# Attention probabilities copied between strips of partitions: 32 rows of 4 KB against 32 rows of four 1 KB pieces

## The reference, cut to what matters

```
xn = layernorm(x)                                  # x: 8 x 1024 x 256, f32
q, k, v = split(einsum('bse,ehd->bshd', xn, w_qkv))  # 16 heads of 64
logits = einsum('bqhd,bkhd->bhqk', q, k) / 8, masked to k <= q
out = einsum('bhqk,bkhd->bqhd', softmax(logits), v)
result = x + einsum('bshd,hde->bse', out, w_out) + moe_ffn(xn)   # 8 experts, top 2
```

## Time and profile before

| | |
|---|---|
| median of 3 runs | 3329.88 us (3329.76 to 3335.65) |
| profiled execution, its own time | 3331.94 us |
| its span, first to last instruction | 3330.1 us |
| mean granted TensorE clock | 0.977 of full speed |
| TensorE busy | 3097.9 us (93%) |
| VectorE, ScalarE, GpSimd busy | 63%, 55%, 48% |
| attention stage | from about 945 us to the end |

### The profile page before, as it was taken

How to read it: one execution, slowest core, us unless ns; L and a number is a source line. 1 busy time by engine, 2 the same in 40 slices (tenths; PEclk the granted TensorE clock), 3 DMA queues, 4 the chain that set the end, 5 groups by cost and what they waited for, 6 DMA issues and landing times.

```text
span 3330.1 us, 62693 instructions
## 1 busy us (share of the span) xinstructions
PE 3097.9 (93%) x21140; PEld 2555.3 (77%) x21141; DVE 2094.2 (63%) x5279; ACT 1840.2 (55%) x4180; POOL 1605.0 (48%) x2256
## 2 busy tenths in 40 slices
PE   5489999999969999999999999999999999999997
PEld 3479998999957777777777777777777777777775
DVE  6844344444337677667766777777776776666665
ACT  3344444455426566656655666666665665556553
POOL 2132222122036565665556666666666655655553
PEclk9799999999979999999999999999999999999998
DMA  6122222112045656656565655656565565555553
GB/s 202 34 73 75 74 72 69 62 59 74 30 117 136 147 140 152 147 136 152 141 146 136 158 139 143 157 146 145 139 162 143 137 155 141 142 131 147 128 134 88
DMA packets 246206, 408.82 MB, mean 123 GB/s; under 512 B 69713, under 2 KB 170129, under 8 KB 245905
## 3 DMA queue, kind: packets, MB, share of 16 engines
q1 hardware_dynamic: 221328, 337.80, 40.4%
q0 software_dynamic: 24576, 67.14, 7.8%
HBM read 102.80 MB, written 33.55 MB: 41 GB/s over the span
## 4 chain that ended last, share of the span: by engine, by line
PE 29%; DVE 19%; SPq 14%; DMA 9%; issue 2%; POOL 0%; ACT 0%; DVEq 0%; POOLq 0%
SPq L1081 14%; PE O L1260 12%; PE S L1224 10%; DMA pT<-squares 8%; DVE squares L1385 8%; DVE S L1406 7%; PE T L1236 4%; DVE res L1372 2%; PE W L1181 2%; DVE negm L1406 1%; DVE ol L1390 1%; PE S L1148 1%; DMA ql<-kk 0%; DVE rinv L1351 0%; DMA kk<-qq 0%
## 5 line engine op out<-in xcount | busy, mean ns | idle before, releaser
L1485 POOL TENSOR_SCALAR pr<-pr,rinv 128x128 f32<-128x128 f32 (+7 forms) x1024 | 765.3, 748 | 868.6 <-DVE rinv L1351 861.9
L1304 ACT ACTIVATE pr<-S,negm 128x128 f32<-128x128 f32 (+7 forms) x1024 | 761.1, 743 | 716.9 <-DVE negm L1406 704.5
L1406 DVE CUSTOM_DVE_ANT_0 S<-S,late 128x128 f32<-128x128 f32 (+7 forms) x1024 | 777.3, 759 | 504.9 <-PE S L1224 504.8
L1260 PE MATMUL O<-pT,vv 128*64 128x256 f32 (+1 forms) x5120 | 587.6, 373 | 97.1 <-DMA pT<-squares 94.8
L1224 PE MATMUL S<-kk,qq 128*128 128x256 f32 (+2 forms) x1536 | 591.1, 385 | 13.7 <-DMA qq<-qq 8.7
L1260 PEld LDWEIGHTS O<-pT,vv 128*64 128x64 f32 x5120 | 348.3, 140 | 298.2 <-DMA pT<-squares 109.7
L1224 PE MATMUL S<-kk,ql 128*128 128x256 f32 (+2 forms) x1536 | 517.3, 344 | 0.0
L1236 PE MATMUL T<-ident,pr 128*128 128x128 f32 x2688 | 418.5, 272 | 0.3 <-POOL pr L1485 0.3
L799 DVE TENSOR_TENSOR hl<-h,hh 128x512 fp32r<-128x512 f32 x256 | 190.8, 746 | 317.1 <-ACT hh L762 317.1
L758 ACT ACTIVATE h<-pH,b1c 128x512 f32<-128x512 f32 x256 | 176.0, 687 | 367.6 <-PE pH L688 355.5
L1224 PEld LDWEIGHTS S<-kk,qq 128*128 128x128 f32 x1536 | 289.9, 189 | 115.0 <-issue 70.8
(11 more groups left out here) (163 smaller groups left out, 6383.9 us busy)
## 6 DMA issues: line engine op xcount, KB each, us to landing
pT<-squares SPq DMA_DIRECT2D x768, 128.0 KB, 3.7
ql<-kk SPq DMA_DIRECT2D x256, 256.0 KB, 4.7
kk<-qq SPq DMA_DIRECT2D x128, 256.0 KB, 2.8
qq<-qq SPq DMA_DIRECT2D x128, 256.0 KB, 3.0
pT<-squares POOLq DMA_DIRECT2D x256, 128.0 KB, 3.9
y<-yb SPq DMA_DIRECT2D x128, 128.0 KB, 1.7
wr<-in_L_attn_w_qkv SPq DMA_DIRECT2D x128, 128.0 KB, 2.9
x<-in_L_attn_x SPq DMA_DIRECT2D x16, 512.0 KB, 5.4
```

What stands on the lines that cost most here:

```text
L1260: ins = e.matmul(O[hs, a:GQ], vv[n // 2 % 2][:, kt, vs], turned_p, start=(kt == 0), stop=(kt == KT - 1))
L1304: e.activation(pr[i][:, 0:w], S[s % 2][:, off:off + w], ACT.Exp, bias=negm[:, i:i + 1], scale=-1.0, accum_out=rsum[:, i:i + 1]).then_inc(e ...
L1406: e.tensor_tensor_reduce(masked, masked, late[:, SEQ - w:], 1.0, -MASKED, ALU.add, ALU.min, negm[:, i:i + 1]).then_inc(negmax.sem, 1)
L1485: e.tensor_scalar(pr[i][:, 0:width(s)], pr[i][:, 0:width(s)], rinv[:, i:i + 1], 1.0, ALU.mult, ALU.mult).then_inc(scaled.sem, 1)
```

## The change

Both sides of the strips get another order of dimensions inside a partition. Before, `squares` and `wide` are [strip index, x, tile of keys, 32], where x = 2 * head + tile of queries (4 values), so a strip's row is one run of 4 KB. Now x stands outside of the strip index. A strip's row is then four pieces of 1 KB, 4 KB apart, in the source as in the destination. The places, the number of DMAs, the bytes, the queues and all waits are the same. The transposes of VectorE write to the new places, and TensorE's reads for group 3 have the two dimensions (tile of queries, strip) in one, since their steps now match.

```
-        wide = ....rearrange("p (a x r) -> p a x r", x=4, a=QUARTERS)
+        wide = ....rearrange("p (x a r) -> p x a r", x=4, a=QUARTERS)

-        sq = sb("squares", [P, QUARTERS, 4, QT, BL])
+        sq = sb("squares", [P, 4, QUARTERS, QT, BL])

-        wide_of = lambda h, kt, t: wide[:, :, 2 * h + t:2 * h + 2, kt * BL:(kt + 1) * BL].rearrange("p a t i -> p t a i")
+        wide_of = lambda h, kt, t: wide[:, 2 * h + t:2 * h + 2, :, kt * BL:(kt + 1) * BL].rearrange("p t a i -> p (t a) i")

         def strip(a, b):
             to, of = slice(b * BL, (b + 1) * BL), slice(a * BL, (a + 1) * BL)
-            return wide[to, a].rearrange("p x r -> p (x r)"), sq[of, b].rearrange("p x k i -> p (x k i)")
+            return wide[to, :, a, :], sq[of, :, b].rearrange("p x k i -> p x (k i)")

-                e.transpose(sq[:, :, x % 2 * 2 + x // 2, 0:KT, :],
+                e.transpose(sq[:, x % 2 * 2 + x // 2, :, 0:KT, :],
                             pr[...]....rearrange("p (k b i) -> p b k i", b=QUARTERS, i=BL))
```

More of the change, by code:

```diff
@@ L885, in attention_and_sum @@
         pT = [[t[:, h] for t in (pT_even, pT_odd)] for h in range(2)]
-        wide = pT_odd[:].rearrange("p h k q -> p (h k q)").rearrange("p (a x r) -> p a x r", x=4, a=QUARTERS)
-        sq = sb("squares", [P, QUARTERS, 4, QT, BL])
+        wide = pT_odd[:].rearrange("p h k q -> p (h k q)").rearrange("p (x a r) -> p x a r", x=4, a=QUARTERS)
+        sq = sb("squares", [P, 4, QUARTERS, QT, BL])
         pr = [sb(f"pr{i}", [P, SEQ]) for i in range(RING)]
```

## The result

The changed kernel takes 3362.22 us (median of 4 runs, 3359.04 to 3372.53) against 3331.77 us: ratio 1.0095, 95% interval 1.007 to 1.012. It is slower by about 30 us. Its profiled execution has a span of 3357.2 us, 27.1 more than before.

What follows compares the result with a forecast made beforehand. The strips' landing in a closed loop of 64 units was taken as the bound; 0.27 us a unit gave 17.3 us, with the clock 20.3, so 3352.2 us profiled and 3350 as forecast. Range: 3304 to 3415.

Steps and rivals of the forecast that it cites:

- the sum of 0.27 us a unit: Strips' landing, each of 64 units: 0.17 us for transfers plus 0.1 us for GpSimd's issues, 17.3 us slower in all.
- GpSimd's issues: 4 a unit at 522 ns each, perhaps growing toward an indirect row's 1060 ns; bounds 0 and 2.2 us, taken 0.1 us.
- TensorE's reads and VectorE's transposes: Group 3's scattered reads cost next to nothing and the transposes' written runs stay long, so both change by 0.
- SyncE's issues: 12 strip issues a unit: no change to 1.0 us less, by L152's 507 ns against 592; taken as 0.
- The transfers: Strip packets of 4 KB become four of 1 KB; only uncontended ones cost more, 0.17 us a unit, bounds 0 and 1.4.
- The clock: TensorE's group 3: longer waits bring 2 more units at the lower clock, 1.7 us each, 3 us in all.
- the signs that I named: Trace after: 73,728 more packets on q1, packets' engine share up 1 to 3% of the burst, landing 11.8 to 12.1 us.
- no change: Rival: transfers wait for the shared limit alone and GpSimd's issue does not grow; 3330 us, chance 0.20.
- The faster one: Rival: SyncE's issue interval falls from 0.63 to 0.55 us and shortens the burst, 0.4 us a unit; 3304 us, chance 0.23.
- The much slower one: Rival: every strip packet grows in proportion, 1.4 us a unit, with more clock dips; priced at 3430 us, chance 0.15.

Runs made afterwards that it cites:

- the pair on SyncE: All 16 strips on SyncE's queue, none on GpSimd's, with the layout of before and with the changed one: 1.0126 and 1.0212 against the kernel before.
- before_ports: Kernel before with SyncE's strips reordered so that those beside GpSimd's differ from them in the halves read and written; 0.9974.
- ports_early: Kernel before with GpSimd's strips issued one step (about 1.6 us) earlier and SyncE's strips reordered against them; 0.989, 3298.52 us.
- after_early: Arrangement of ports_early with the changed layout; 1.0093 against the kernel before.

## Why the prediction came out as it did

I forecast 3350 us and slower; it is 3362, ratio 1.0095 where I had 1.006. The range and the direction held, and the loop was read rightly: what the strips' landing lost, TensorE's wait gained. That the sum of 0.27 us a unit came near the measured 0.33 is in part luck: 0.1 of it stood for GpSimd's issues, which cost nothing, and the issues of SyncE, which I took as 0, cost up to 0.27. The terms:

- *TensorE's reads and VectorE's transposes, 0.* Right: 2.81 us and 1225 ns.
- *SyncE's issues, taken as 0 with bounds of 0 and 1.0 us less.* This step failed. The true value lay outside the bounds: 0.09 us at the first packet and 0.016 us per interval more. I had read L152 (four pieces, 507 ns) as the price of the shape, but its transfers come from HBM, to 128 partitions, and L1081's go from SBUF to SBUF, between 32; which of these differences counts no run separates. I had also called the engines the bound because of the queue behind the twelfth issue. In the first strips the issue is what they wait for: one lands every 0.63 us, at the interval of the issues. With one queue this term is the whole loss, 0.32 us a unit, shown by the pair on SyncE.
- *The transfers, 0.17 us.* Half right. With one queue the pieces cost the engines nothing more (87.2% for 1.40 MB, 87.4% for 1.42). But in the stretch that two queues share the engines are full, and there, where I had expected pieces to cost nothing, they do: 235 GB/s for 243, and 242 for 264 in the order of before_ports. I had put the cost at the free packets. The issue gives at most 0.09 + 11 x 0.016 = 0.27 us, so of the 0.65 us in the order of before_ports about 0.4 are left, and of the 0.86 in that of ports_early about 0.6. In the arrangement of the change, issue and packets together make 0.33 us; SyncE's packets took 279 ns per 4 KB against 262, 6% more, where I had 1 to 3%.
- *GpSimd's issues, 0.1 us.* Nothing. L1452 went to 585 ns, not toward the 1060 of the indirect row, and GpSimd's last strip lands 9.9 us after SyncE's first issue in the median (10.2 before), ahead of SyncE's.
- *The clock, 3 us.* 3.4 us, with 12 slow groups against 9; with one profile of each kernel a difference of three is weak. One of after, with idle before it:

```profile
3196.79 4.40 PE L1260 MATMUL O<-pT,vv 128*64 128x256 f32 x24 [2.67 <-DMA pT<-squares]
```

It is the kind of row: from 3196.80 to 3200.20 the granted clock was 0.52. In the experiments 13 to 20 slow groups go with 12.5 to 13.0 us from first issue to group 3, and 3 with 11.63; so the clock adds to most losses here, but not to all: the pair with one queue has 13 and 13.

Of the signs that I named, the packets came (73,728 more on SyncE's queue), and the 12.34 us of the unit shown lie above my 11.8 to 12.1; they are 0.68 more than before, just inside the 0.7 beyond which I had called myself wrong. The mean over the units moved by 0.33.

Of the rivals, no change is excluded by the interval; its ground, that the engines take no longer for pieces, holds where SyncE's queue is alone, but the landing came later even there. The faster one had the sign of the issue wrong. The much slower one, 1.4 us a unit, did not come; the pair ports_early and after_early, in another arrangement, comes nearest to it with 0.86.

Open: how much of the 0.33 us in the arrangement of the change is the issue and how much the shared stretch. The twelfth issue starts 0.76 us later there, more than the 0.27 of the issues' own, and the landing is only 0.33 later, so the two do not simply add. Open too is what makes the late issues longer; and whether in the shared stretch the pieces cost by themselves, or because SyncE's 1 KB packets take turns with packets of 4 KB on GpSimd's queue. Both fit all pairs. A kernel with pieces on one of the two queues alone was not run.

## What to carry to other kernels

Cut a row of an SBUF to SBUF copy into pieces only for a reason that pays: here each of 12 issues on the critical chain got longer, and a stretch with two busy queues lost 3% to 8% of its rate. Price a DMA's issue from a row that is like it in source, destination and partitions, not only in the number of pieces. When a burst of copies is on the chain, look first at when each queue begins: starting GpSimd's four copies one step earlier and reordering the others gave 1.1% together, and only with whole rows.

## What was unexpected

- SyncE's interval of 0.634 us between strips stayed when an increment was put between them; the issue instruction shrank from 592 to 539 ns instead.
- The minimum issue of L1081 is 507 ns with one dimension, 585 ns with two, whether the pieces are 2 KB or 1 KB, and whichever side is cut.
- GpSimd's queue moves the 1 KB pieces as packets of 4 KB (its count stayed at 24576), SyncE's moves each piece as a packet (221328 became 295056).
- Longer waits bring more slow groups, but not one by one: after 2.58 us of idle the group took 2.81 us, after 2.21 us 4.48.
